# Four depthwise-convolution steps moved behind the four output tiles of each first-sweep stage

## The reference, cut to what is computed

```python
xn = layernorm(x)
q, k, v = split(xn @ Wqkv)                    # 8 heads of 128
tele = softmax over k at distances 0,1,2,4,...,4096 of q.k/sqrt(128), times v
conv = causal depthwise convolution of v, 7 taps per channel (conv_w)
low  = linear attention with elu(q)+1, elu(k)+1 and v over all positions
attn = xn + (tele + conv + low) @ Wo
ffn  = sigmoid(xr @ W_r.T) * (relu(xk @ W_k.T)**2 @ W_v.T)   # xr, xk: mixes of xn and xn one row earlier
y    = x + attn + ffn
```

## Time and profile before

| what | value |
|---|---|
| median of 10 runs | 2177.51 us (2163.96 to 2220.16) |
| profiled execution, its own time | 2186.91 us |
| span of its slowest core (5) | 2185.3 us |
| spans of all cores | 2136.6 to 2185.3 us |
| PE busy | 66% |
| DVE busy | 56% |
| ACT busy | 34% |
| POOL busy | 5% |

### The profile page before, as it was taken

How to read it: one execution, slowest core, us unless ns; L and a number is a source line. 1 busy time by engine, 2 the same in 40 slices (tenths; PEclk the granted TensorE clock), 3 DMA queues, 4 the chain that set the end, 5 groups by cost and what they waited for, 6 DMA issues and landing times.

```text
span 2185.3 us, 32445 instructions; the slowest of 8 cores (2136.6 to 2185.3 us)
## 1 busy us (share of the span) xinstructions
PE 1444.4 (66%) x10400; PEld 822.6 (38%) x10400; DVE 1226.8 (56%) x1968; ACT 740.8 (34%) x976; POOL 117.9 (5%) x137
## 2 busy tenths in 40 slices
PE   0069688688785887868869435556565666658484
PEld 0024333333333343333434222425353544536281
DVE  0176286485794866848667464545454453526263
ACT  0024123142241422414224133434444443526252
POOL 0001101001010010110101000000000000000000
PEclk9997677689787997979979657777787877879697
DMA  8711130220412303113031360404040403031210
GB/s 145 110 68 49 36 129 30 87 104 3 145 49 61 123 11 127 67 43 135 16 106 49 96 154 10 146 10 145 11 145 11 136 21 135 21 125 31 96 50 39
DMA packets 75228, 168.07 MB, mean 77 GB/s; under 512 B 38080, under 2 KB 38208, under 8 KB 69952
## 3 DMA queue, kind: packets, MB, share of 16 engines
q1 hardware_dynamic: 59632, 100.98, 14.5%
q0 software_dynamic: 15440, 65.02, 10.8%
HBM read 113.55 MB, written 67.11 MB: 83 GB/s over the span
## 4 chain that ended last, share of the span: by engine, by line
PE 47%; DVE 15%; DMA 14%; ACT 11%; issue 11%; SPq 1%; DVEq 1%; POOL 0%; ACTq 0%; POOLq 0%
PE PS L466 6%; PE PS L540 6%; PE PS L597 5%; PE PS L568 5%; DVE s_cv L281 5%; PE PS L889 4%; PE PS L1045 3%; PE PS L1048 3%; PE PS L938 3%; PE PS L893 3%; PE PS L941 3%; PE PS L627 3%; DMA s_vr<-vt_sp 2%; DMA s_wq<-wqkv 2%; DMA s_p<-p_sp 2%
## 5 line engine op out<-in xcount | busy, mean ns | idle before, releaser
L466 PE MATMUL PS<-s_xnfm,s_wq 128*128 128x512 bf16 x1536 | 379.5, 412 | 28.8 <-ACT s_qk L489 25.1
L281 DVE SCALAR_TENSOR_TENSOR s_cv<-s_vh,s_cw,s_cv 128x512 bf16<-128x512 bf16 x384 | 322.4, 840 | 42.6 <-DVE s_cv L281 2.7
L909 DVE RECIPROCAL s_rr<-PS 128x512 f32<-128x512 f32 x64 | 214.9, 3358 | 124.0 <-PE PS L893 123.9
L956 ACT ACTIVATE s_er<-PS,s_con 128x768 bf16<-128x768 f32 (+5 forms) x256 | 226.3, 887 | 161.3 <-PE PS L941 160.7
L466 PEld LDWEIGHTS PS<-s_xnfm,s_wq 128*128 128x128 bf16 x1536 | 158.7, 104 | 246.4 <-issue 124.5
L938 PE MATMUL PS<-s_q,s_kr 128*128 128x128 bf16 x1288 | 185.9, 230 | 94.8 <-DMA s_q<-q_sp 80.4
L941 PE MATMUL PS<-s_id,s_mlog 128*128 128x128 bf16 x1288 | 186.8, 231 | 0.0
L889 PE MATMUL PS<-s_er,s_vr 128*128 128x128 bf16 x1288 | 118.8, 225 | 83.8 <-ACT s_er L956 52.4
L938 PEld LDWEIGHTS PS<-s_q,s_kr 128*128 128x128 bf16 x1288 | 132.8, 104 | 101.8 <-issue 99.6
L392 PE MATMUL PS<-s_id,s_xnb 128*128 128x128 bf16 x256 | 29.4, 278 | 157.7 <-DVE s_st L378 125.7
L941 PEld LDWEIGHTS PS<-s_id,s_mlog 128*128 128x128 bf16 x1288 | 133.3, 104 | 0.0
(11 more groups left out here) (99 smaller groups left out, 1875.1 us busy)
## 6 DMA issues: line engine op xcount, KB each, us to landing
s_xa<-x SPq DMA_DIRECT2D x32, 512.0 KB, 4.4
s_xb<-x SPq DMA_DIRECT2D x32, 512.0 KB, 3.8
p_sp<-s_p POOLq DMA_DIRECT2D x32, 512.0 KB, 4.6
s_p<-p_sp SPq DMA_DIRECT2D x32, 512.0 KB, 8.5
y<-s_p SPq DMA_DIRECT2D x32, 512.0 KB, 3.3
q_sp<-s_qk POOLq DMA_DIRECT2D x8, 1024.0 KB, 4.2
k_sp<-s_qk POOLq DMA_DIRECT2D x8, 1024.0 KB, 4.2
vt_sp<-s_vt POOLq DMA_DIRECT2D x8, 1024.0 KB, 8.1
```

Source lines behind the costliest of these rows:

```text
L281: cinc(e.scalar_tensor_tensor(s1_cv[:, ch, :], src, s_cw[:, ch, j:j + 1], s1_cv[:, ch, :], ALU.mult, ALU.add))
L466: last = e.matmul(bank(bsel, 0, 512), s1_wq[:, kc, 128 * m:128 * (m + 1)], s1_xnfm[:, kc, 1:513], start=(kc == 0), stop=(kc == 7), skip_gr ...
L909: cinc(e.reciprocal(s2_rr[:, 512 * half:512 * half + 512], PS[:, 512 * (6 + half): 512 * (6 + half) + 512]))
L956: return e.activation(s2_er[:, eslot, 0:128 * n], src, AF.Exp, bias=s_con[:, 0:1], scale=s_con[:, 1:2])
```

## The change

The four convolutions of heads 4 to 7 leave the loop over row tiles. In DVE's list they now stand behind the fourth output tile step. Nothing is added or removed: the same instructions run with the same waits, and only DVE's order differs. The lists of the other engines are as before.

```diff
             W("gpsimd", (lambda st, rt, g=g: lambda e: e.dma_start(
                 out=p_sp[st, :, rt, :], in_=s1_p[:, rt % 2, :]))(st, rt),
                 waits=[("dve", pas_arr[rt]), ("d_p", 16 * g)], inc="d_p", amt=16)
-
-            emit_conv_head(st, 4 + rt)
+        for ch in (4, 5, 6, 7):
+            emit_conv_head(st, ch)
         pas_last[st] = pas_arr[3]
```

## The result

The changed kernel takes 2254.0 us (median of 13 runs, 2232.5 to 2273.5). The kernel before takes 2177.8 us over all its runs. The ratio is 1.034, with a 95% interval of 1.030 to 1.038, so the change costs 74 us (66 to 82). The forecast was 2240 us, which is 62 more.

What follows compares the result with a forecast made beforehand. DVE was taken to bound the stage boundaries, with PE having time to spare. Six boundaries at 7.6 us (45.6), 7.6 out of stage 6 and 9.6 out of stage 7 add 62.8 to 2177.5: 2240 us, range 2205 to 2275.

Steps and rivals of the forecast that it cites:

- Step 1: Stage boundary: PE gets its next 24 groups 5.8 us earlier, costed at nothing.
- Steps 2 and 3: Stage boundary: DVE waits 4.0 us for spill 0, then for spill 1; delay 7.6 us, at six boundaries 45.6 us.
- The formula: Delay per boundary: the two spill landing times plus 2.75, less 3 x 2.05, that is their sum less 3.4.
- clock term: Boundary out of stage 6: PE stalls before groups 8 to 11, then a slow stretch at half clock loses 2.6 us.
- Out of stage 6: Boundary after stage 6: spills of 4.4 and 4.0 us delay 5.0, plus 2.6 for the slow PE stretch: 7.6 us.
- Out of stage 7: Start of the second sweep's chain: spills of 5.2 and 7.8 us give a delay of 9.6 us.
- Crowded spills: Rival: loads crowd both spills at all eight boundaries, each takes 7.8 us; 100 us more, 2278; chance 0.12.
- quick spills: Rival: both spills at each boundary take the uncrowded 2.9 us; 22 us more, 2199; chance 0.08.
- No change: Rival: DVE's idle time is taken up by overlooked slack; 2177 us; chance 0.03.
- faster: Rival: PE's head start of 5.8 us counts at seven boundaries, 41 us, giving 2137; chance 0.03.
- the bounds worked out before it: Lowest and highest seen spill times at eight boundaries: 31 and 98 us, 2209 and 2275; with clock term 2278.

Runs made afterwards that it cites:

- e5: Changed kernel with four buffers each for output tiles and x rows, so no spill or x load is waited for; ratio 1.000 to the kernel before.
- e4: Changed kernel with convolution 4 put behind 3, and 5 to 7 behind the last W_v multiply; ratio 0.967 to the kernel before.
- e6: Changed kernel with convolutions 4 to 7 moved to mid-stage and four buffers each for output tiles and x rows; 2075.2 us, 0.954 to the kernel before.
- e3: Same instructions reordered: output tile steps 0 and 1, convolutions 4 and 5, steps 2 and 3, convolutions 6 and 7; ratio 1.0007 to the kernel before.
- e2: Changed kernel with the two layernorm loads behind tile 3's x load held until the fourth output tile step; ratio 1.026 to the kernel before.

## Why the prediction was right, and what was mis-sized

*The bound.* Right. DVE ended the boundary: with its transfers' waits taken away (e5) the time is that of the kernel before, and with its convolutions taken away (e4, e6) it is 3.3% and 4.6% less.

*Step 1, PE's head start is worth nothing.* Right: e3 gives it without any spill wait and measures 1.0007. It isn't free of cost everywhere. Out of stage 6, where the V copies are held as in e5, e3 took 126.7 us in the median of the cores, against 123.4 before.

*Steps 2 and 3, the two spill waits.* Right in place and in kind. The formula, sum of the two landing times less 3.4, gives 7.2 + 5.4 - 3.4 = 9.2 for stage 2, where DVE's stretch grew by 9.8. Three terms were off.

- The landing time of spill 0 was too short. I kept the 5.3 us of the earlier trace rows, on the ground that the same x load lies beside it. In the changed kernel it took 7.2 in stage 2, 6.6 to 7.5 in stages 1 to 5 of core 5, and 6.7 in the mean of stages 0 to 5 and eight cores. I had let the earlier loads bear on spill 1 alone. e2 keeps two of the three away, and the mean is 5.7.
- Spill 1 was somewhat too long: 5.7 forecast, 5.4 in stage 2, 3.9 to 6.2 in stages 1 to 5, 5.0 in the mean.
- The formula has nothing for the time from the landing of spill 0 to the issue of spill 1. It was 0.5 us each time (555.58 to 556.10 in stage 2).

The means give 6.7 + 5.0 - 3.4 + 0.5 = 8.8 us, and the delay of output tile step 3 was 8.9 where 7.6 was forecast. The errors of the two spills go opposite ways, so that the sum came so close is in part luck. It also depends on the core: over all eight boundaries the delays come to 64 us in the mean of cores 0 to 3 and to 73.5 us on core 5, where the forecast without its clock term had 60.2. The measured 74 us is that of the slowest core of each execution.

*Out of stage 6.* Spill 0 took 6.5 us (forecast 4.4) and spill 1 took 2.9 (forecast 4.0), so the sum was nearly right. The clock term of 2.6 us shows up in the mean, but not on every core. Core 5 took 130.5 us here against 124.2 before, 6.3 more, and its two waits (5.1 and 1.3) are all of that. Over eight cores the boundary grew by 7.9 us, the delay of output tile step 3 was 5.9, and 2.0 are left. e5, which has the stalls but no spill wait, shows 1.9 us on core 5. There the granted clock was 0.63 from 1118 to 1122 us, behind the stall of 4.28, and 1.00 from 1122 on. No run takes the low clock away and keeps the stalls, so what it costs by itself is not shown.

*Out of stage 7.* Spills of 7.8 and 6.4 us against 5.2 and 7.8: a delay of 11.7 measured, 9.6 forecast. Again it is spill 0, 2.6 us longer; spill 1 was 1.4 shorter, and the 0.5 between them is missing here too.

*The rivals.* Crowded spills came about half true, for the first spill. The quick spills didn't come. DVE was mostly idle while spill 0 was in flight, and it took longer than before (6.7 us against 4.8 in the mean). With no x load sent beside them, in e5, the spills of stages 0 to 5 were quick: spill 0 took 3.1 us in the mean and spill 1 took 3.3, and spills 2 and 3 of stage 2, issued under convolutions, took 2.9 each:

```profile
p_sp<-s_pf POOLq DMA_DIRECT2D x1, 512.0 KB, 2.9
```

So the loads beside the spills set their time, and DVE's convolutions don't lengthen them. The Trainium skill (SBUF — State Buffer, "SBUF: two separate sides") ties the lock on descriptors to DVE's 2-port modes, and says that `tensor_tensor`, which has no such mode, didn't stall a transfer. The 2.9 us agree with that, since six of a convolution's eight instructions are of the kind with two SBUF inputs (`scalar_tensor_tensor`, L281). I had read the rule too widely when I let it cover a whole convolution. "No change" and "faster" are excluded by the interval.

*The range.* It was stated up to 2275 us, though the bounds worked out before it reach 2278; the reason is not given.

*Span against median.* Core 5's span grew by only 46.6 us between the two profiled executions. Its first output tile step began at 267.1 before and at 248.3 after, 18.8 us earlier, in a part that the change doesn't touch. It was the kernel before that was late there: its cores 4 and 5 reached that step at 262.7 and 267.1, all others of both kernels between 242 and 252. From its first output tile step to that of stage 7 core 5 took 966.3 us before and 1023.3 after, and from there to the end 951.9 and 960.3. That is 65 us from the same point, and 55 to 99 on cores 0 to 5. A single span isn't the measure of a change of this size.

## What to carry to other kernels

Work between two uses of a double buffer is cover for the transfer that frees the buffer. Before regrouping, take the landing time of that transfer and subtract what will still lie in between; where two such transfers are issued one behind the other's landing, their times add up. If the waiting engine is the one that ends the stage, the rest is paid in full at every turn. When an instruction moves up, look also at which loads it releases, since they go out earlier and slow the very transfer that is now waited for. And if an engine ends one part of a stage but idles in another (17 us here), moving its work there is worth more than any order within the part: 3.3% alone, and 4.6% with deeper buffers.

## What the runs showed of the hardware that was not expected

DVE's convolution is much slower while GpSimd squares the feed-forward values. These are timeline rows of the kernel before, core 5: six instructions of one convolution with POOL at rest, and the same six beside POOL's.

```profile
629.34 5.04 DVE L281 SCALAR_TENSOR_TENSOR s_cv<-s_vh,s_cw,s_cv 128x512 bf16<-128x512 bf16 x6
...
648.87 8.93 DVE L281 SCALAR_TENSOR_TENSOR s_cv<-s_vh,s_cw,s_cv 128x512 bf16<-128x512 bf16 x6
...
649.30 1.21 POOL L580 TENSOR_TENSOR s_xr<-s_xr 128x512 bf16<-128x512 bf16 x1 [0.69 <-ACT s_xr L576]
```

That is 8.93 us for 5.04. POOL was in a tensor_tensor for about 1.04 of every 1.73 us there. I take it to cost nothing here, since DVE idles later in the same stage (17 us before L679), but no run tests that. The slower convolution agrees with what the Trainium skill says (SBUF — State Buffer, "SBUF: two separate sides") of a port that a DVE operation with two SBUF inputs and a GpSimd operation that reads SBUF can't use at once. No run here separates the port from other causes.
